# Values of two pairs of heads made in one product of 256 moving columns, and raw weights kept apart

## The reference

```
latent_kv = x @ w_kv_down                     # (2, 2048, 128)
kv = latent_kv @ w_kv_up                      # keys and values of 16 heads, 64 each
q = (x @ w_q).reshape(B, T, 16, 64)
att = softmax(where(causal, einsum('bqhd,bkhd->bhqk', q, k) * 64 ** -0.5, -inf))
y = einsum('bhqk,bkhd->bqhd', att, v).reshape(B, T, 1024)
return y @ w_out
```

## Time and profile before

| | |
|---|---|
| median of 3 runs | 2170.82 us (2165.53 to 2171.48) |
| the profiled execution | 2168.69 us, of which the span is 2167.3 us |
| mean granted TensorE clock | 0.978 of full speed |
| PE, DVE, ACT, POOL busy | 93%, 62%, 51%, 66% of the span |
| first layers and entry | about 0 to 300 us |
| attention | about 300 to 2070 us, some 107 us a pair |
| last mixer | about 2030 us to the end, its start beside the last units |

### The profile page before, as it was taken

How to read it: one execution, slowest core, us unless ns; L and a number is a source line. 1 busy time by engine, 2 the same in 40 slices (tenths; PEclk the granted TensorE clock), 3 DMA queues, 4 the chain that set the end, 5 groups by cost and what they waited for, 6 DMA issues and landing times.

```text
span 2167.3 us, 35663 instructions
## 1 busy us (share of the span) xinstructions
PE 2013.0 (93%) x13104; PEld 1264.6 (58%) x13104; DVE 1340.9 (62%) x2711; ACT 1101.0 (51%) x2226; POOL 1426.3 (66%) x812
## 2 busy tenths in 40 slices
PE   5998578999999999999998999999999999999899
PEld 3666445556565656565655565656565665565466
DVE  5888646576656565656565656576656565656453
ACT  4776534445444444444464444445454444444575
POOL 0333214778787878787867687878787878687822
PEclk9999789999999999999999999999999999999999
DMA  3000000000000000000000000000000000000001
GB/s 114 1 1 1 8 8 6 11 19 11 19 11 19 11 19 11 19 11 19 11 19 11 18 11 18 11 19 11 18 11 18 11 19 11 18 11 11 25 25 59
DMA packets 25787, 37.03 MB, mean 17 GB/s; under 512 B 6544, under 2 KB 14864, under 8 KB 25616
## 3 DMA queue, kind: packets, MB, share of 16 engines
q1 hardware_dynamic: 25616, 34.76, 5.0%
HBM read 30.02 MB, written 4.46 MB: 16 GB/s over the span
## 4 chain that ended last, share of the span: by engine, by line
PE 71%; DVE 16%; ACT 5%; POOL 3%; issue 3%; DMA 0%; ACTq 0%; DVEq 0%; POOLq 0%; SPq 0%
PE heads_out L833 20%; PE beside L652 11%; PE two_heads L790 8%; PE scores L652 7%; PE scores L813 5%; PE scores L819 5%; PE scores L817 5%; PE scores L815 5%; DVE part_max L1021 3%; POOL acc L1319 2%; PE beside L844 2%; DVE stats L872 2%; PE beside L798 2%; PE two_heads L652 2%; ACT prob L1234 2%
## 5 line engine op out<-in xcount | busy, mean ns | idle before, releaser
L1319 POOL TENSOR_TENSOR acc<-acc,prob 128x1024 f32<-128x1024 f32 (+3 forms) x512 | 1017.5, 1987 | 195.3 <-ACT prob L1234 138.7
L1234 ACT ACTIVATE prob<-scores 128x512 f32<-128x512 f32 (+3 forms) x1280 | 579.4, 539 | 649.3 <-DVE scores L1031 327.4
L1021 DVE TENSOR_REDUCE part_max<-two_heads 128x2 f32<-128x1024 f32 x384 | 468.8, 1221 | 315.6 <-PE two_heads L790 315.3
L833 PE MATMUL heads_out<-prob,V 128*64 128x512 f32 (+3 forms) x2560 | 544.9, 547 | 0.0
L1018 DVE CUSTOM_DVE_ANT_0 two_heads<-two_heads,mask 128x128 f32<-128x128 f32 (+3 forms) x512 | 242.0, 514 | 188.4 <-PE two_heads L790 188.3
L790 PE MATMUL two_heads<-k_hi,q_hi 64*128 64x512 f32 (+3 forms) x1280 | 273.8, 423 | 56.9 <-DVE part_max L1021 27.1
L833 PEld LDWEIGHTS heads_out<-prob,V 128*64 128x64 f32 x2560 | 156.9, 137 | 225.3 <-issue 203.2
L790 PEld LDWEIGHTS two_heads<-k_hi,q_hi 64*128 64x128 f32 x1280 | 120.5, 184 | 249.2 <-issue 143.0
L813 PE MATMUL scores<-q_hi,k_hi 64*128 64x512 f32 (+3 forms) x1280 | 235.9, 364 | 1.2 <-ACT neg_max L1221 0.8
L819 PE MATMUL scores<-neg_max,sel 64*128 64x512 f32 (+3 forms) x1280 | 235.4, 362 | 0.0
L817 PE MATMUL scores<-q_lo,k_hi 64*128 64x512 f32 (+3 forms) x1280 | 235.4, 362 | 0.0
(11 more groups left out here) (294 smaller groups left out, 3077.0 us busy)
## 6 DMA issues: line engine op xcount, KB each, us to landing
rden<-rden_rows SPq DMA_DIRECT2D x128, 128.0 KB, 2.9
wP_raw<-wPair SPq DMA_DIRECT2D x16, 384.0 KB, 3.1
X<-u SPq DMA_DIRECT2D x8, 512.0 KB, 8.9
out<-X SPq DMA_DIRECT2D x8, 512.0 KB, 2.9
den<-den_rows SPq DMA_DIRECT2D x64, 4.0 KB
rden_rows<-inverse SPq DMA_DIRECT2D x64, 4.0 KB, 1.3
wA_sb<-wA SPq DMA_DIRECT2D x1, 768.0 KB, 7.0
wFa<-wF SPq DMA_DIRECT2D x1, 768.0 KB, 7.8
```

The source lines that it names most:

```text
L833: made = pe.matmul(heads_out[head(h), x0:], V[(idx - j + c) % NVS][:, tt, head(h)], prob[step % NPROB][:, h, x0:], start=t == 0, stop=t == ...
L1021: made = ve.reduce_max(part_max[:, t, :, c:c + 1], two_heads[:, :, 0:width], AX.X)
L1234: ac.activation(prob[step % NPROB][:, h, x0:], bank(task, h)[:, x0:], ACT.Exp).then_inc(empty(task, h)[0], 1)
L1319: po.tensor_tensor(total[:, :, x0:], total[:, :, x0:], new[:, :, x0:], ALU.add).then_inc(acc_ok, 1)
```

## The change

Values are made for two pairs of heads at once. The 8 pairs of a sequence become 4 groups of two; `value` now has a number `vn` (group times 4 plus block) and a half: each half takes 2 of the block's 4 tiles, with 256 moving columns, in 2 by 3 = 6 matmuls into one bank. There are 32 blocks of 2 halves. All values of a group are made for its first pair, and its second pair makes none. `V` has 5 slots, each of twice the size.

The weights are three tensors now: queries and keys (384 columns, two buffers), values (256 columns for a group, one buffer), output (256 columns, two buffers). Each raw weight is loaded into the memory that its `_lo` part will take (`weights`), and the subtraction is done in place. The tasks `fetch_pair`, `fetch_values`, `fetch_out` issue the DMAs ahead of `load_pair`, `load_values`, `load_out`; the first pair's weights are loaded at the start of the program. To make room, `att_xn` has 2 buffers, `neg_max` 3, and the reciprocal of the denominators is taken in place.

```diff
-NKS, NVS = 7, 6
+NKS, NVS, NMAX = 7, 5, 3
@@ ENTRY
-         (9, "updated"): [("key", 0), ("query", 0)], (9, "mixed"): ["maximum", ("turn_tiles", 0, 6), "maximum", ("value", 0)],
+         (9, "updated"): [("key", 0), ("query", 0)], (9, "mixed"): ["maximum", ("turn_tiles", 0, 6), "maximum", ("value", 0, 0), ("value", 0, 1)],
@@ Plan.need
+        elif kind == "value":
+            _, vn, half = task
+            n, j = divmod(vn, NBLK)
+            self.need("latent", n // (NPAIR // 2), j)
+            self.need("load_values", n)
+            if ("values_lo", n) in self.chores:
+                self.chore(("values_lo", n))
...
@@ Plan.fillers
-            out.append((max(start[first] + 4 if j >= 2 else start[first] - LEAD - 8, at + TPB * j - 14 - early), at + TPB * j - 3 - early, ("value", idx)))
+            if p % 2 == 0:
+                for half in range(2):
+                    out.append((max(start[first] + 2 if j else start[first] - LEAD - 8, at + TPB * j - 14), at + TPB * j - 2 + half, ("value", self.value_of(b, p, j), half)))
@@ Plan.attention
-        loads = [(start_of - LEAD - 14, ("load_pair", n)) for n, start_of in enumerate(self.start[::NBLK])]
-        loads += [(start_of - 10, ("load_out", n)) for n, start_of in enumerate(self.start[::NBLK])]
+        for n, first in enumerate(self.start[::NBLK]):
+            loads += [(max(2, first - 16), ("fetch_out", n)), (max(6, first - 10), ("load_out", n))]
+            if n:
+                loads += [(max(2, first - LEAD - 20), ("fetch_pair", n)), (first - LEAD - 14, ("load_pair", n))]
+            if n and n % 2 == 0:
+                loads += [(first - 40, ("fetch_values", n // 2)), (first - 34, ("load_values", n // 2))]
@@ build
+        def weights(where, name, shape):
+            hi = sb(where, name + "_hi", shape, F32R)
+            with ExitStack() as before:
+                raw = sb(before, name + "_raw", shape)
+            return hi, sb(where, name + "_lo", shape, F32R), raw
...
-            V = slots("V", 2, NVS, [P, TPB, P])
+            V = slots("V", 1, NVS, [P, TPB, 2, P])
@@ tensor_program, value
-                    for t in range(TPB):
-                        tc = slice(j * BLK + t * P, j * BLK + (t + 1) * P)
-                        made = product(bank(task)[:, t * P:(t + 1) * P], terms((lat_hi[:, tc], lat_lo[:, tc]), wp(n, 3 * P, 4 * P)))
+                    for t in range(2):
+                        tc = slice(j * BLK + (2 * half + t) * P, j * BLK + (2 * half + t + 1) * P)
+                        made = product(bank(task)[:, t * 2 * P:(t + 1) * 2 * P], terms((lat_hi[:, tc], lat_lo[:, tc]), (wV_hi[:, :], wV_lo[:, :])))
@@ vector_program
+                elif kind == "values_lo":
+                    n = task[1]
+                    w.wait_ge(wV_hi_ok, n + 1)
+                    ve.tensor_tensor(wV_lo[:, :], wV_raw[:, :], wV_hi[:, :], ALU.subtract).then_inc(wV_ok, 1)
...
-                    ve.reciprocal(inverse[:, :], den[:, :]).then_inc(inverted, 1)
+                    ve.reciprocal(den[:, :], den[:, :]).then_inc(inverted, 1)
@@ sync_program
+            sp.dma_start(wQK_raw[0][:, :], wQuery[0]).then_inc(wQK_in, 16)
+            sp.dma_start(wV_raw[:, :], wValue[0]).then_inc(wV_in, 16)
...
-                    w.wait_ge(wP_ok, 2 * n)
-                    w.wait_ge(wO_ok, n)
-                    sp.dma_start(wP_raw[:, :], wPair[n % NPAIR]).then_inc(wP_in, 16)
+                    if n >= 2:
+                        for made in ("query", "key"):
+                            w.wait_ge(*full((made, (n - 1) * NBLK - 1)))
+                    sp.dma_start(wQK_raw[n % 2][:, :], wQuery[n % NPAIR]).then_inc(wQK_in, 16)
+                elif kind == "fetch_values":
+                    n = task[1]
+                    w.wait_ge(*full(("value", n * NBLK - 1, 1)))
+                    sp.dma_start(wV_raw[:, :], wValue[n % (NPAIR // 2)]).then_inc(wV_in, 16)
```

More of the change, by code:

```diff
@@ L325, in need @@
             _, idx, t = task
[L326 removed]
+            self.need("value", self.value_of(*UNITS[idx][:2], t // TPB), t % TPB // 2)
         self.add(*task)
@@ L536, in build @@
         lat_lo = sb(early, "lat_lo", [P, T], F32R)
-        axn = [sb(early, f"att_xn{i}", [P, C]) for i in range(4)]
-        kd_hi = sb(early, "kd_hi", [P, CH, RANK], F32R)
-        kd_lo = sb(early, "kd_lo", [P, CH, RANK], F32R)
-        wP_raw = sb(early, "wP_raw", [P, WPC])
-        kd_raw = wP_raw[:, 0:CH * RANK].rearrange("p (c r) -> p c r", c=CH)
+        axn = [sb(early, f"att_xn{i}", [P, C]) for i in range(2)]
+        kd_hi, kd_lo, kd_raw = weights(early, "kd", [P, CH, RANK])
+        wQK_hi, wQK_lo, wQK_raw = [[x] for x in weights(early, "wQK0", [P, WQK])]
+        wV_hi, wV_lo, wV_raw = weights(early, "wV", [P, 2 * P])
         with ExitStack() as tail_scope:
@@ L567, in build @@
             q_hi, q_lo = slots("q_hi", 2, NQ, [P, BLK], F32R), slots("q_lo", 2, NQ, [P, BLK], F32R)
-            neg_max = slots("neg_max", 2, NQ, [P, BLK], F32R)
-            V = slots("V", 2, NVS, [P, TPB, P])
-            wP_hi, wP_lo = slots("wP_hi", 1, 2, [P, WPC], F32R), slots("wP_lo", 1, 2, [P, WPC], F32R)
+            neg_max = slots("neg_max", 2, NMAX, [P, BLK], F32R)
+            V = slots("V", 1, NVS, [P, TPB, 2, P])
+            for slot, x in zip((wQK_hi, wQK_lo, wQK_raw), weights(ph, "wQK1", [P, WQK])):
+                slot.append(x)
+            wO_hi, wO_lo, wO_raw = zip(*[weights(ph, f"wO{i}", [P, C]) for i in range(2)])
             acc = slots("acc", 1, 2, [P, 2, BLK])
@@ L641, in attention_memory @@
         def attention_memory(w):
-            for kind in ("query", "key", "value", "turn_max"):
+            for kind in ("query", "key", "turn_max"):
                 w.wait_ge(*full((kind, NU - 1)))
-            w.wait_ge(wO_ok, NB * NPAIR)
+            w.wait_ge(*full(("value", NU // 2 - 1, 1)))
         def tensor_program(pe):
@@ L818, in tensor_program @@
                     for h in range(2):
-                        pe.matmul(bank(task, h)[:, x0:], sel[head(h), :], neg_max[i][head(h), x0:], start=False, stop=True).then_inc(full(task, h)[0], 1)
+                        pe.matmul(bank(task, h)[:, x0:], sel[head(h), :], neg_max[idx % NMAX][head(h), x0:], start=False, stop=True).then_inc(full(task, h)[0], 1)
                 elif kind == "weigh":
@@ L826, in tensor_program @@
                         w.wait_ge(*empty(("score", idx, t), h))
-                    w.wait_ge(*empty(("value", idx - j + c)))
+                    vn, p = plan.value_of(*UNITS[idx][:2], c), UNITS[idx][1]
+                    w.wait_ge(*empty(("value", vn, tt // 2)))
                     if t == 0:
@@ L1406 @@
     HD = NH * DH
-    pair = [np.concatenate([halves(wq[:, i:i + P]).reshape(P, CH * P), up[:, i:i + P], up[:, HD + i:HD + i + P],
-                            wo[i:i + P, :]], axis=1) for i in range(0, HD, P)]
+    query = [np.concatenate([halves(wq[:, i:i + P]).reshape(P, CH * P), up[:, i:i + P]], axis=1) for i in range(0, HD, P)]
     arrays = {
```

140 lines of the change are left out of this document (82 added, 58 removed).

## The result

The kernel after takes 2139.28 us in the median of 4 runs (2137.23 to 2141.33), the kernel before on the same chip 2171.15 us (4 runs). The ratio is 0.9863, 95% interval [0.9849, 0.9878]: 1.4% faster; the medians lie 31.9 us apart. Forecast were 2138 us. The profiled execution took 2138.73 us, 30.0 less than the one before, span 2137.4, mean clock 0.977 (before 0.978).

What follows compares the result with a forecast made beforehand. PE was taken to bound attention, busy 104.05 of 106.7 us a pair. From 2168.69 us, 37 off for values, 5 added for POOL and 1 for the entry gave 2137.7, predicted as 2138 us, range 2124 to 2158.

Steps and rivals of the forecast that it cites:

- Values on PE: Attention's value products: half as many matmuls, each costing nearly the same, save 37 us, at most 41.
- The rival of an unhidden load: Value matmuls: stationary load not hidden, 0.17 us per 256-column matmul, gain only 21 us, about 2155 us; smaller-gain chance 0.13.
- POOL in the last block: Last block of each pair: POOL can't fully follow quicker PE, losing 0.3 us a pair, 5 us over 16; bounds 0 and 19.
- The entry: Program's entry: PE waits 1.5 us for `wV_lo` at the first value; net +1 us, bounds 0 and +3.
- Elsewhere: Later weight splits on DVE, fetches and smaller buffers: nothing for each; 8 us kept for the range if splits delayed maxima.
- Waits for maxima: PE's waits in narrow diagonal steps unchanged; its waits between 330 and 1970 us grow by 5 us or less.
- The sum: Whole program: 2168.69 - 37 + 5 + 1 = 2137.7 us, 2138 predicted for the median, 1.5% less.
- The clock rival: Attention's last blocks: PE idles behind POOL and its clock drops, about 2200 us; chance 0.05, shared with another long wait.

Runs made afterwards that it cites:

- b1_wide: Kernel before, its 12 matmuls per value moving 256 columns in place of 128 (values wrong): 2177.84 us, ratio 1.0038.
- the light POOL: Kernels after and before, POOL adding only one of two heads from each unit's third step on (output wrong): 2106.56 us after, 2149.52 before.
- c3_std: Kernel after, the last statistics' eps added inside ACT's square root in place of a separate DVE operation: 2134.97 us, ratio 0.9843.
- a4_fill: Kernel after, side work put ahead of the second maximum in each unit's last, narrow iteration: 2122.13 us, ratio 0.978.
- b4_fill: Kernel before, side work put ahead of the second maximum in each unit's last, narrow iteration: 2160.52 us, ratio 0.9962.
- c5_last: Kernel after, output scaling and splitting of all four units of the last pair on DVE, two more than before the edit: 2134.88 us, ratio 0.9841.
- a1_narrow: Kernel after, each value half made by 12 matmuls of 128 columns in place of 6 of 256: 2179.03 us, ratio 1.0042.
- a3_early: Kernel after, low part of the first value weights made right behind the first key and query: 2135.17 us, ratio 0.9837.

## Why the prediction was right, step by step

**Values on PE: right.** The spacing is 0.112 and 0.12 us in the kernels themselves, there are 384 value matmuls (in the list of lines 108 + 20 for each of three terms), and the count alone is worth 39.8 us for the 37 forecast, inside the bound of 41. PE's busy time fell by 38.8 us. The surplus fits halves that took 0.82 us, where half a `project`'s 0.90 was put in. The rival of an unhidden load is dead: b1_wide would have had to cost 45 us and cost 8. The section that the prediction cites for it, "The mechanism" in the Trainium skill's "TensorE: Matmul & The Clock Gate", names a second case beside the other group of rows, a load into the background weight buffer; the prediction left it out, and the spacings fit it.

**POOL in the last block: right in the common pairs, missing for the last.** 0.3 us a pair were forecast and the light POOL shows 0.2, a difference of small numbers from four profiles. ACT's exponential waits for POOL as before at the place shown in the earlier trace rows (2.68 us in both); in the whole span its waits for POOL's additions grew from 53.1 to 66.7 us, as foretold. But the step took the same loss for all 16 pairs. In the last pair, with nothing of a next pair to fill PE, the whole chain hangs on POOL: it should have given 4 x 0.58 = 2.3 us and gave -0.4, by the estimate 1.3 us gained in the work and 1.7 lost to the clock. The chain by engine couldn't show this; a window on the last pair would have: there PE was busy for 92.0 of 102.2 us.

**The entry: right in place and size.** PE waited 1.25 us for `wV_lo` (1.5 forecast), and 4.40 for 4.78 us for the low part of the weights of queries and keys. The subtraction took 0.42 us with POOL idle, the short duration that was put in.

**"Elsewhere", costed at nothing: wrong in one place.** Later value weights cost nothing that shows; PE waited 0.9 us once for `neg_max` in a filler, as in the kernel before, and never for a `V` slot. But a statistics operation on DVE, which the change doesn't touch, came to start 0.11 us behind the start of an addition on POOL and no more in the gap between two. c3_std shows that without it the pair is 4.3 us shorter: 1.2 us are the stall, the rest goes with the half clock behind it. The Trainium skill, "SBUF — State Buffer", section "SBUF: two separate sides", says that the port pair shared by DVE and GpSimd is an exclusive lock for whole instructions. The trace agrees: the small operation ended with the addition. The page gives the lock to DVE instructions with two operands in SBUF or in a two-port mode; this one has a single operand, so by that page it must have been of the second kind, which no run here shows apart.

**Waits for maxima: outside the forecast's limit of 5.** They grew by 7.6 us between 330 and 1940 us, 2.2 of it at the place of the stalled operation (2.53 for 0.29 us). The prediction said that the narrow steps were unchanged, which holds for the maxima; but less of PE's work stands around them, so DVE is awaited longer. That the same reordering takes 13.9 us of these waits after the change and 8.8 before (a4_fill against b4_fill) fits this; that the shorter value work alone does it wasn't isolated.

**The sum.** 37 - 5 - 1 = 31 us were forecast and 31.9 measured (26 to 33 by the interval). That it came out so close is in part luck, since errors of opposite sign met: the count was 3 us better and the first pair ended 4.9 us earlier in its profile (the clock, see c5_last), against 4.3 us at pair 10 and 2.7 in the last. The 9 us of "the rest of the change" in a1_narrow are spread: its first pair ended 5.0 us later than before's (453.8 us), of which the halves of two pairs made in it are some 3 (its other first pairs take 110.3 us, before 107.0); pair 10 is 0.9 us more over its like than before; the rest is the entry and waits for DVE and POOL that aren't separated further.

**The clock rival: wrong in size, not in kind.** The clock stayed at 1.00 in the common pairs, so the fall in every pair didn't come. But PE did idle in one piece and the clock did fall, in pair 10 beside a wait for DVE and in the last pair beside one for POOL. Pairs 1 to 15 had 27.3 us at half level for 13.7 before, about 7 us by the estimate, which the forecast had at nothing. The first pair, with 10.2 us less, hid 5 of them, and the mean of the span (0.977 for 0.978) shows neither.

## What to carry to other kernels

Where full-height float32r matmuls of 128 and 256 moving columns start 0.112 and 0.119 us apart, count matmuls, not columns: find products that share the stationary operand and run them as one. Read a per-stage gain in every stage, the last pass of a pipeline included: work that fills the bound engine there is missing, and another engine sets the time. A change that shifts the order by a fraction of a microsecond can put a small VectorE operation under a long GpSimd one; a table of durations per repetition (here per pair) finds the odd one at once. Put the granted clock of each repetition beside its duration before you give a difference to an edit: a run of the same code elsewhere in the program, as a3_early here, is such a check.

## What was not expected of the hardware

A VectorE instruction can last as long as the GpSimd instruction beside it. The product of mean and reciprocal, with two SBUF operands, took 0.65 us in the kernel after and 0.28 in c3_std (0.18 in a1_narrow, with no addition beside it). The timelines of DVE and POOL, first after, then c3_std:

```profile
1492.05 0.65 DVE L949 SCALAR_TENSOR_TENSOR minus_mean<-mean_var,rstd 128x16 f32<-128x16 f32 x1
```
```profile
1491.40 1.27 POOL L1377 TENSOR_TENSOR oT<-oT,rden 128x512 f32<-128x512 f32 x1
```
```profile
1492.75 0.28 DVE L953 SCALAR_TENSOR_TENSOR minus_mean<-mean_var,rstd 128x16 f32<-128x16 f32 x1
```
```profile
1490.60 2.40 POOL L1385 TENSOR_TENSOR acc<-acc,prob 128x1024 f32<-128x1024 f32 x1 [0.17 <-POOL acc L1385]
```

Both times it ends 0.03 us behind the GpSimd instruction (1492.70 and 1492.67; 1493.03 and 1493.00), as the one-operand addition of eps did. The `RECIPROCAL` of the same 16 columns took 0.25 us in both, in c3_std in the middle of POOL's addition: it doesn't wait.

The mean clock of one stretch behind the entry (300 to 350 us) was 0.91 and 0.80 in two kernels that are identical up to there; their first pairs were at half level for 68.3 and 78.5 us and ended 5.0 us apart. Deep in the program, at pair 10, the same tasks with the same wait of 2.5 us for DVE were followed by 6.8, 3.4 or no us at half level (after, c5_last and a3_early, a4_fill).
